# Decay table times span states in three rounded products, with table and states in two parts and one table for both tiles

## The chip, the cores and the metric

The kernel runs on one core of one Trainium2 chip. The metric is the device time in microseconds (us), the median of several runs. Beside it stands one execution that the hardware profiler recorded; all rows below come from that one.

## What is computed

Eight sequences of 1024 tokens with 512 channels pass two layers, both added to their input. The part that matters here is the second layer's decayed sum: eight causal moving averages with their own decay, each over gated values with its own modulation, blended per channel.

```python
ctx = causal_ema(x, tau_ctx)
gate_in = jnp.concatenate([x, ctx], axis=-1)
wg = jax.nn.sigmoid(jnp.einsum('btc,ec->bte', gate_in, Wg) + bg)
gated = x * wg
...
mod = 0.5 + jax.nn.sigmoid(jnp.einsum('bth,dh->btd', h1, Wn2) + bn2)
traces = jax.vmap(lambda tau, m: causal_ema(gated * m[..., None], tau))(tau_raws, jnp.moveaxis(mod, -1, 0))
blend_w = jax.nn.softmax(blend, axis=0)
temporal = jnp.einsum('dbtc,dc->btc', traces, blend_w)
gate = jax.nn.sigmoid(jnp.einsum('btc,ec->bte', temporal, Wtemp) + btemp)
soma = jax.nn.gelu(jnp.einsum('btc,ec->bte', x, Wsoma) + bsoma, approximate=False)
out = jnp.einsum('btc,ec->bte', soma * gate, Wout)
```

## The kernel before

The work is cut into 16 tiles of 512 tokens, two per sequence: the even one is the first half, the odd one the second half. A loop over slots k from -1 to 16 is written out on every engine. In slot k the tile k-1 is finished ("prev": temporal gate, output product, norm), tile k is in the middle ("cur"), and tile k+1 goes through the first layer ("next"). Each engine runs its instructions in the order in which `slot(k)` writes them, and semaphores join them. So the order is hand-written, and no scheduler moves anything.

Large products are done with both operands split in two rounded parts of type fp32r, high and low: `split_product` issues high by high, high by low and low by high. The high part is made by ACT (a copy that rounds), the low part by DVE (value minus high part).

The decayed sum of a tile of four blocks of 128 tokens has two parts, which meet in the same PSUM bank `Tp[b % 2]`, for block b:

- `within_spans(b, hh)` (L1011): within spans of 32 tokens. DVE's `products(b, hh, c)` (L761) multiplies the gated values, repeated over the partitions in `grep`, by blend weights into `U`. PE multiplies that by the decay matrices `Arep`.
- `from_before(b)` (L1020): what the span states bring in from before. `span_states` on PE (L993) writes one state per span and decay (16 x 8 = 128 rows) into the bank `smp`. DVE's `span_states` (L776) weights them by `w_jd` into `V`. PE multiplies the table `Epow` by `V` as plain fp32, one product for each block.

`tile_state` (L1026), in even tiles alone, makes the state that goes over to the odd tile. ACT copies it to `V[1][96:128]` (L514). There are two `V` buffers and 2 x 4 blocks of `Epow`: even and odd tiles have their own.

Then, for block b, ACT copies `Tp` out (`trace`, L492), PE transposes it (`trace_by_channels`, L1032), ACT makes the high part (`trace_high`, L436) and DVE the low one (`trace_low`, L649). With `trace_low(3)` the next slot's `temporal_gate` can begin; in a profile that is the product `ring<-seq_hi,Wtemp_hi`.

`grep` is loaded from memory, where SP's queue stores the gated values and reads them back four times per block (`repeat_spans`, L328). There are two buffers, so the load of block 3 waits until DVE has done the last product of block 1:

```python
                    if b >= 2:
                        sp.wait_ge(U_ready, upto(PIECES, k, 4 * (b - 2) + 3))
```

Of the kernel before, what the change touches and what calls it, by code (L numbers as in the profile page):

```python
# [4 lines left out]
P = 128  # L5
BATCHES, SEQ, C = 8, 1024, 512
A = 128
D = 8
# [3 lines left out]
NB = TOK // P  # L12
NC = C // P
L = 32
# [3 lines left out]
SPANS = TOK // L  # L18
LEVELS = 10
# [13 lines left out]
AT_EMASK = AT_EBITS + 5  # L33
# [7 lines left out]
def cond_resid_kernel(nc, x, xc, ids, w1, w2, b1, b2, g0, be0, wg, wn1, wsoma, wtemp, wout, wn2,  # L41
# [10 lines left out]
    with ctx:  # L52
        def sb(name, shape, dt=F):
            return ctx.enter_context(nc.sbuf_tensor(name, shape, dt))
# [10 lines left out]
        def sem(name):  # L65
            return ctx.enter_context(nc.semaphore(name))
# [31 lines left out]
        w_jd = sb("w_jd", [P, C])  # L98
        Dpow = sb("Dpow", [P, NH, L])
        Rpow = sb("Rpow", [P, NI, D])  # L100
        Epow = sb("Epow", [P, 2 * NB, P])
        Eend = sb("Eend", [P, 2 * (L - D) + D])

        grep = [sb(f"grep_{n}", [P, NI, C]) for n in range(2)]
        x_t = grep[0]
# [16 lines left out]
        V = [sb(f"V_{n}", [P, C]) for n in range(2)]  # L122
        soma, soma_lo = sb_two_ways("soma", [P, NC, TOK])
        stats0, stats1 = (V[0][:, at:at + 6 * NB].rearrange("p (b s) -> p b s", s=6)
                          for at in (128, 160))
        mv0, mv1 = (V[0][:, at:at + 2 * NB].rearrange("p (b s) -> p b s", s=2) for at in (192, 208))
# [12 lines left out]
        alpha = V[0][:, 0:LEVELS * ALS].rearrange("p (n a) -> p n a", a=ALS)  # L139
        alpha_1 = V[0][:, 128:128 + LEVELS * ALS].rearrange("p (n a) -> p n a", a=ALS)  # L140
        Qpow, Tpow = V[0][:, 256:288], V[0][:, 288:320]
        factors = g[:, :, :].rearrange("p n c -> p (n c)")[:, 0:5 * 4 * L].rearrange("p (n a t) -> p n a t", n=5, a=4)
        factors_s = V[0][:, 320:320 + 5 * D].rearrange("p (n d) -> p n d", n=5)
        factors_e = V[0][:, 384:389]
        blend_c = V[1][:, 0:NC * D].rearrange("p (n d) -> p n d", d=D)
        blend_s = V[1][:, 64:64 + NC]

        blend_x = ema.rearrange("p n t -> p (n t)")[:, 0:3 * NC * P].rearrange("p (a n c) -> p a n c", a=3, n=NC)

# [32 lines left out]
        split_lo = [sem(f"split_lo{n}") for n in range(6)]  # L182
        setup_step = sem("setup_step")
        blend_ready = sem("blend_ready")
        tables_ready = sem("tables_ready")
        sg_ready, ln1_step = sem("sg_ready"), sem("ln1_step")
        y_ready, ln0_step, x1_ready = sem("y_ready"), sem("ln0_step"), sem("x1_ready")
# [6 lines left out]
        rstd0_ready, rstd1_ready = sem("rstd0_ready"), sem("rstd1_ready")  # L194
        res_ready = sem("res_ready")
        xb2_ready, xbeta_ready, x1b_ready = sem("xb2_ready"), sem("xbeta_ready"), sem("x1b_ready")

        def upto(per_tile, tile, j):

            return tile * per_tile + (j + 1)  # L200
# [214 lines left out]
        def _(act):  # L415
            def split(n):

                act.wait_ge(ld_split[n], 16)
                hi, lo, raw = halves[n]
                nc.scalar.activation(hi, raw, ACT.Identity).then_inc(split_hi, 1)  # L420

            def slot(k):
                has_prev, has_cur, has_next = parts_of(k)

                def soma_gelu(e):
                    act.wait_ge(full["soma"], upto(4, k, e))
                    nc.scalar.activation(soma[:, e, :], bank_of("soma", k, e)[:, :], ACT.Gelu,
                                         bias=col[:, 1 + e:2 + e]).then_inc(soma_ready, 1)
# [57 lines left out]
                def open_gate(b):  # L486
                    act.wait_ge(pre_ready, upto(4, k, b))
                    nc.scalar.activation(g[:, b, :], g[:, b, :], ACT.Sigmoid).then_inc(sig_ready, 1)  # L488

                def trace(b):  # L490
                    act.wait_ge(full["T"], upto(4, k, b))
                    nc.scalar.activation(T_sb[b % 2][:, :], Tp[b % 2][:, :], ACT.Identity).then_inc(T_ready, 1)  # L492

                if has_cur:
                    open_gate(0)
                    act.wait_ge(m_pre, upto(1, k, 0))
                    nc.scalar.activation(m_nat, m_nat, ACT.Sigmoid).then_inc(msig_ready, 1)
                    if k == 0:
                        split(4)
                        split(5)  # L500
                    for b in range(1, NB):
                        open_gate(b)
                    soma_gelu(1)
                    trace(0)
                    soma_gelu(2)
                    trace(1)
                    trace_high(0)
                    trace(2)
                    trace_high(1)
                    soma_gelu(3)  # L510
                    if not k & 1:

                        act.wait_ge(full["carry"], k // 2 + 1)
                        nc.scalar.activation(V[1][96:128, :], smp[96:128, :], ACT.Identity).then_inc(carry_ready, 1)  # L514
                if k == -1:
                    split(0)
                    split(1)
                    split(2)
                if has_cur:
                    trace(3)  # L520
                if has_next:
                    x1_high(0)
                if has_cur:
# [21 lines left out]
        def _(dve):  # L545
            steps = [0]

            def link(ins):

                steps[0] += 1  # L550
                ins.then_inc(setup_step, 1)
                dve.wait_ge(setup_step, steps[0])
# [31 lines left out]
            def decay_tables():  # L584
# [18 lines left out]
                link(V_.memset(Eend[:, :], 0.0))  # L603
# [4 lines left out]
                for n in range(1, 5):  # L608
# [5 lines left out]
                V_.tensor_scalar(Eend[:, L - D:L], con[:, AT_EMASK:AT_EMASK + D], power_e, None, ALU.mult)  # L614
                V_.tensor_tensor(Qpow, power[:, 3, :], con[:, AT_QMASK:AT_QMASK + 32], ALU.mult)
                link(V_.tensor_scalar(Tpow, power[:, 0, :], alpha[:, 0, AL_JD:AL_JD + 1], None, ALU.mult))
                V_.tensor_tensor(Epow[:, :, :].rearrange("p x (i t) -> p (x i) t", t=L), Qpow.unsqueeze(2).to_broadcast([P, 32, L]),
                                 Tpow.unsqueeze(1).to_broadcast([P, 32, L]), ALU.mult)
# [5 lines left out]
            def slot(k):  # L624
# [146 lines left out]

                def span_states():

                    rows = slice(0, P - D if odd else P)
                    dve.wait_ge(full["S"], upto(1, k, 0))
                    V_.tensor_tensor(V[odd][rows, :], smp[rows, :], w_jd[rows, :], ALU.mult).then_inc(V_ready, 1)  # L776

                if has_cur:
                    if k == 0:
# [22 lines left out]
                                     ALU.mult).then_inc(A_ready, 1)  # L802
                    if k == 0:
                        split(4)
                    gate_logits(2)
                    gated(2)
                    dve.wait_ge(A_ready, upto(1, k, 0))
# [40 lines left out]
        def _(pe):  # L848
# [14 lines left out]
            def slot(k):  # L863
# [99 lines left out]
                def modulation():  # L963

                    pe.wait_ge(h1_ready, upto(1, k, 0))
                    if has_prev:
                        pe.wait_ge(V_ready, upto(1, k - 1, 0))
                        if odd:
                            pe.wait_ge(carry_ready, (k + 1) // 2)
# [44 lines left out]

                def from_before(b):

                    if b == 0 and k == 0:
                        pe.wait_ge(tables_ready, 1)
# [141 lines left out]
```

## Time and profile before

| | us |
|---|---|
| median of 3 runs | 1423.78 |
| lowest and highest | 1421.12, 1425.09 |
| the profiled execution, its own time | 1424.65 |
| its span in the profile | 1422.9 |

| engine | busy us | share of the span | instructions |
|---|---|---|---|
| PE (matmul) | 1344.8 | 95% | 7836 |
| DVE | 1010.4 | 71% | 1493 |
| ACT | 512.6 | 36% | 812 |
| POOL | 379.0 | 27% | 295 |

The profiled execution is 0.87 us above the median. The TensorE clock granted over the span was 0.987 of full speed. PE's busy time overlaps with itself, since matmuls are pipelined: a product of 128x512 is shown with 0.39 us while the next begins 0.23 us after it. A plain fp32 product of that size shows as two matmul records.

### The profile page before, as it was taken

What the parts mean: (1) busy time and instruction counts of PE and PEld (TensorE: products, weight loads), DVE (VectorE), ACT (ScalarE), POOL (GpSimd) and SP (SyncE); (2) the same over time, 40 slices, a digit from 0 to 9 for tenths busy, and PEclk for the clock granted to TensorE, in tenths of its full rate; (3) what the DMA queues carried; (4) which work ended last, traced back from release to release, by engine and by line L of the source; (5) the groups of instructions that cost most, each with busy time, mean ns of one, the idle gap of its engine ahead of it and who ended that gap; (6) DMA issues with size and microseconds to landing.
All of it is one profiled execution on the core that took longest, in us unless ns stands there. A gap on an engine that the chain in (4) does not pass through costs nothing.

```text
span 1422.9 us, 19538 instructions
## 1 busy us (share of the span) xinstructions
PE 1344.8 (95%) x7836; PEld 974.6 (68%) x7836; DVE 1010.4 (71%) x1493; ACT 512.6 (36%) x812; POOL 379.0 (27%) x295
## 2 busy tenths in 40 slices
PE   3599999999999999999999999999999999999995
PEld 2376857677586776858677685767758677686854
DVE  6967677676777867777776767767677786767463
ACT  2324234252333424234242433425233343423422
POOL 4414223041330514124041422304123051421102
PEclk8799999999999999999999999999999999999999
DMA  7345361735528173361715636173451816334250
GB/s 254 118 119 185 91 176 48 209 106 138 158 70 226 39 180 117 111 195 68 200 58 148 185 85 182 45 202 117 132 165 61 229 45 167 130 105 133 74 134 30
DMA packets 91484, 186.22 MB, mean 131 GB/s; under 512 B 9858, under 2 KB 14594, under 8 KB 87298
## 3 DMA queue, kind: packets, MB, share of 16 engines
q1 hardware_dynamic: 91394, 184.98, 44.8%
q8 instruction: 62, 1.02, 0.3%
q14 instruction: 28, 0.23, 0.1%
HBM read 134.61 MB, written 50.33 MB: 130 GB/s over the span
## 4 chain that ended last, share of the span: by engine, by line
PE 74%; DVE 9%; ACT 4%; DMA 4%; issue 3%; POOL 1%; SPq 1%; POOLq 0%; DVEq 0%
PE ring L859 56%; PE Tp L1011 6%; DVE U L761 5%; PE Tp L1020 4%; PE ring L852 3%; PE Tp L859 2%; DMA g_blocks<-g_f 2%; DVE seq_lo L649 2%; ACT T_sb_f L492 2%; PE smp L974 1%; DVE x1T_lo L631 1%; PE smp L993 1%; ACT seq_hi L436 1%; DMA grep<-g_blocks 1%; SPq L328 1%
## 5 line engine op out<-in xcount | busy, mean ns | idle before, releaser
L761 DVE TENSOR_TENSOR U<-grep,w_qs 128x1024 f32<-128x1024 f32 x256 | 298.4, 1219 | 6.6 <-DMA grep<-g_blocks 6.6
L382 POOL TENSOR_TENSOR x<-grep,b_row 128x512 f32<-128x512 f32 x64 | 80.5, 1289 | 603.3 <-DMA grep<-in_x 603.3
L1011 PE MATMUL Tp<-U,Arep 128*32 128x256 f32 x2048 | 146.5, 386 | 15.3 <-DVE U L761 14.8
L766 DVE TENSOR_TENSOR g_f<-ring,bg_row 128x512 f32<-128x512 f32 x64 | 44.2, 691 | 133.8 <-PE ring L859 133.8
L488 ACT ACTIVATE g_f<-g_f 128x512 f32<-128x512 f32 x64 | 40.5, 632 | 264.9 <-DVE g_f L766 264.8
L1011 PEld LDWEIGHTS Tp<-U,Arep 128*32 128x32 f32 x2048 | 52.7, 109 | 104.3 <-DVE U L761 44.8
L391 POOL TENSOR_TENSOR grep<-grep,beta_row 128x512 f32<-128x512 f32 x64 | 80.9, 1296 | 156.1 <-DMA grep<-x_tiles 156.1
L859 PE MATMUL ring<-seq_hi,Wtemp_hi 128*128 128x512 f32 x256 | 106.8, 417 | 8.5 <-DVE seq_lo L649 8.5
L492 ACT ACTIVATE T_sb_f<-Tp 128x512 f32<-128x512 f32 x64 | 38.2, 597 | 209.8 <-PE Tp L1020 209.8
L859 PE MATMUL ring<-Wg_hi,seq_hi 128*128 128x512 f32 x256 | 100.7, 393 | 9.1 <-DVE Wg_r L560 9.1
L859 PE MATMUL ring<-x1T_hi,Wsoma_hi 128*128 128x512 f32 x256 | 106.7, 417 | 0.0
L859 PE MATMUL ring<-Wg_hi,x1T_hi 128*128 128x512 f32 x256 | 103.4, 404 | 0.0
L859 PE MATMUL ring<-Wout_hi,g_r 128*128 128x512 f32 x256 | 99.8, 390 | 3.2 <-DVE soma_r L657 3.2
L859 PE MATMUL ring<-Wg_r,seq_hi 128*128 128x512 f32 x256 | 100.5, 393 | 0.0
L859 PE MATMUL ring<-Wg_hi,seq_lo 128*128 128x512 f32 x256 | 100.5, 393 | 0.0
L859 PE MATMUL ring<-x1T_hi,Wsoma_r 128*128 128x512 f32 x256 | 100.4, 392 | 0.0
L859 PE MATMUL ring<-Wg_hi,x1T_lo 128*128 128x512 f32 x256 | 100.0, 391 | 0.0
L859 PE MATMUL ring<-seq_hi,Wtemp_r 128*128 128x512 f32 x256 | 99.9, 390 | 0.0
L859 PE MATMUL ring<-x1T_lo,Wsoma_hi 128*128 128x512 f32 x256 | 99.9, 390 | 0.0
L859 PE MATMUL ring<-Wg_r,x1T_hi 128*128 128x512 f32 x256 | 99.7, 390 | 0.0
L859 PE MATMUL ring<-seq_lo,Wtemp_hi 128*128 128x512 f32 x256 | 99.7, 389 | 0.0
L859 PE MATMUL ring<-Wout_r,g_r 128*128 128x512 f32 x256 | 99.6, 389 | 0.0
(151 smaller groups left out, 2823.6 us busy)
## 6 DMA issues: line engine op xcount, KB each, us to landing
grep<-g_blocks SPq DMA_DIRECT2D x256, 256.0 KB, 4.4
grep<-in_xc SPq DMA_DIRECT2D x16, 1024.0 KB, 7.4
grep<-in_x SPq DMA_DIRECT2D x16, 1024.0 KB, 8.1
x_tiles<-x SPq DMA_DIRECT2D x16, 1024.0 KB, 7.6
g_blocks<-g_f SPq DMA_DIRECT2D x64, 256.0 KB, 4.6
grep<-x_tiles SPq DMA_DIRECT2D x16, 1024.0 KB, 4.8
out<-U SPq DMA_DIRECT2D x64, 256.0 KB, 2.0
gamma_row<-in_g SPq DMA_DIRECT2D x9, 256.0 KB, 7.6
```

Source lines behind the costliest of these rows:

```text
L328: sp.dma_start(grep[b % 2][q * L:(q + 1) * L, :, :], g_dram[b].rearrange("(i s) c -> s i c", i=NI)).then_inc(grep_in[b % 2], 16)
L382: nc.gpsimd.tensor_tensor(new[:, b, :], x_t[:, b, :], b2_row[:, :], ALU.add).then_inc(xb2_ready, 1)
L391: nc.gpsimd.tensor_tensor(x1_back[:, b, :], x1_back[:, b, :], beta1_row[:, :], ALU.add).then_inc(x1b_ready, 1)
L488: nc.scalar.activation(g[:, b, :], g[:, b, :], ACT.Sigmoid).then_inc(sig_ready, 1)
L492: nc.scalar.activation(T_sb[b % 2][:, :], Tp[b % 2][:, :], ACT.Identity).then_inc(T_ready, 1)
L649: V_.tensor_tensor(seq[1][:, :, at], bank_of("tt", k, b)[:, :].rearrange("p (n t) -> p n t", n=NC), seq[0][:, :, at].bitcast(F), ALU.subtr ...
L761: V_.tensor_tensor(U[:, (n + 2) % 4, :, :], grep[b % 2][:, :, at], w_qs[:, hh, at].unsqueeze(1).to_broadcast([P, NI, HC]), ALU.mult).then_ ...
L766: V_.tensor_tensor(g[:, b, :], bank_of("wg", k, b)[:, :], bg_row[:, :], ALU.add).then_inc(pre_ready, 1)
L852: last = nc.tensor.matmul(dst, lhsT(n), rhs(n), start=(n == 0), stop=(n == steps - 1))
L859: last = nc.tensor.matmul(dst, lhsT(a, n), rhs(b, n), start=(first and n == begin and m == 0), stop=(final and n == steps - 1 and m == 2))
L1011: last = nc.tensor.matmul(Tp[b % 2][i * L:(i + 1) * L, at], Arep[:, b * NI + i, hh, :], U[:, (n + 2) % 4, i, :], start=(hh == 0 and c == 0 ...
L1020: nc.tensor.matmul(Tp[b % 2][:, :], Epow[:, odd * NB + b, :], V[odd][:, :], start=False, stop=True).then_inc(full["T"], 1)
```

## The change

`Epow` and `Eend` (now 128 columns wide) are built as plain fp32 and split once, in slots -1 and 0, into high and low parts. Only one set of four `Epow` blocks is kept. DVE weights the span states in place in `smp`; ACT rounds them to `V_hi` (`states_high`), and DVE subtracts (`states_low`) into `V_lo`. `from_before` and `tile_state` become three fp32r products each. The copy of the tile state on ACT stands behind `trace(3)` now, in front of `x1_high(0)`, and DVE's `carry_low` is added at the end of an even tile's slot. The small statistics get a buffer of their own.

```diff
-        Epow = sb("Epow", [P, 2 * NB, P])
-        Eend = sb("Eend", [P, 2 * (L - D) + D])
+        Epow_raw, Epow_lo = sb_two_ways("Epow", [P, NB, P])
+        Epow = [sb("Epow_hi", [P, NB, P], R), Epow_lo]
+        Eend_raw, Eend_lo = sb_two_ways("Eend", [P, P])
+        Eend = [sb("Eend_hi", [P, P], R), Eend_lo]
...
+        def state_rows(tile):
+
+            return slice(0, P - D if tile & 1 else P)
+
+        def earlier_rows(tile):
+
+            return slice(0, P if tile & 1 else P - D)
...
+                def states_high():
+                    rows = state_rows(k)
+                    act.wait_ge(V_ready, upto(1, k, 0))
+                    nc.scalar.activation(V_hi[rows, :], smp[rows, :], ACT.Identity).then_inc(Vhi_ready, 1)
...
                     soma_gelu(1)
+                    states_high()
                     trace(0)
...
                     soma_gelu(3)
-                    if not k & 1:
-
-                        act.wait_ge(full["carry"], k // 2 + 1)
-                        nc.scalar.activation(V[1][96:128, :], smp[96:128, :], ACT.Identity).then_inc(carry_ready, 1)
...
+                    act.wait_ge(tables_ready, 1)
+                    nc.scalar.activation(Epow[0][:, :, :], Epow_raw[:, :, :], ACT.Identity).then_inc(tablehi_ready, 1)
+                    nc.scalar.activation(Eend[0][:, :], Eend_raw[:, :], ACT.Identity).then_inc(tablehi_ready, 1)
                 if has_cur:
                     trace(3)
+                    if not k & 1:
+
+                        act.wait_ge(full["carry"], k // 2 + 1)
+                        nc.scalar.activation(V_hi[96:128, :], smp[96:128, :], ACT.Identity).then_inc(carry_ready, 1)
                 if has_next:
                     x1_high(0)
...
-                    rows = slice(0, P - D if odd else P)
+                    rows = state_rows(k)
                     dve.wait_ge(full["S"], upto(1, k, 0))
-                    V_.tensor_tensor(V[odd][rows, :], smp[rows, :], w_jd[rows, :], ALU.mult).then_inc(V_ready, 1)
+                    V_.tensor_tensor(smp[rows, :], smp[rows, :], w_jd[rows, :], ALU.mult).then_inc(V_ready, 1)
+
+                def states_low():
+
+                    rows = state_rows(k)
+                    dve.wait_ge(Vhi_ready, upto(1, k, 0))
+                    V_.tensor_tensor(V_lo[rows, :], smp[rows, :], V_hi[rows, :].bitcast(F), ALU.subtract).then_inc(Vlo_ready, 1)
+
+                def carry_low():
+
+                    dve.wait_ge(carry_ready, k // 2 + 1)
+                    V_.tensor_tensor(V_lo[96:128, :], smp[96:128, :], V_hi[96:128, :].bitcast(F),
+                                     ALU.subtract).then_inc(carrylo_ready, 1)
...
                     if k == 0:
                         split(4)
+                        dve.wait_ge(tablehi_ready, 2)
+                        V_.tensor_tensor(Epow[1][:, :, :], Epow_raw[:, :, :], Epow[0][:, :, :].bitcast(F),
+                                         ALU.subtract).then_inc(tablelo_ready, 1)
+                        V_.tensor_tensor(Eend[1][:, :], Eend_raw[:, :], Eend[0][:, :].bitcast(F),
+                                         ALU.subtract).then_inc(tablelo_ready, 1)
...
                     products(1, 0, 0)
+                    states_low()
                     products(1, 0, 1)
...
+                if has_cur and not odd:
+                    carry_low()
...
-                    pe.wait_ge(V_ready, upto(1, k, 0))
-                    nc.tensor.matmul(Tp[b % 2][:, :], Epow[:, odd * NB + b, :], V[odd][:, :],
-                                     start=False, stop=True).then_inc(full["T"], 1)
+                    pe.wait_ge(Vlo_ready, upto(1, k, 0))
+                    for m, (a, c) in enumerate(((0, 0), (0, 1), (1, 0))):
+                        last = nc.tensor.matmul(Tp[b % 2][:, :], Epow[a][rows, b, :], V[c][rows, :], start=False, stop=(m == 2))
+                    last.then_inc(full["T"], 1)
...
-                    nc.tensor.matmul(smp[96:128, :], Eend[:, 0:L], V[0][:, :], start=True, stop=True).then_inc(full["carry"], 1)
+                    for m, (a, c) in enumerate(((0, 0), (0, 1), (1, 0))):
+                        last = nc.tensor.matmul(smp[:, :], Eend[a][:, :], V[c][:, :], start=(m == 0), stop=(m == 2))
+                    last.then_inc(full["carry"], 1)
```

On DVE, where an even tile's span states are weighted, before:

```order
L770 TENSOR_TENSOR g_f<-g_f,x_0 128x512
L776 TENSOR_TENSOR V<-smp,w_jd 128x512
L761 TENSOR_TENSOR U<-grep,w_qs 128x1024 x6
L649 TENSOR_TENSOR seq_lo<-ring,seq_hi 128x4x128
L761 TENSOR_TENSOR U<-grep,w_qs 128x1024 x4
```

and now:

```order
L795 TENSOR_TENSOR g_f<-g_f,x_0 128x512
L801 TENSOR_TENSOR smp<-smp,w_jd 128x512
L786 TENSOR_TENSOR U<-grep,w_qs 128x1024
L807 TENSOR_TENSOR V_lo_r<-smp,V_hi_r 128x512
L786 TENSOR_TENSOR U<-grep,w_qs 128x1024 x5
L674 TENSOR_TENSOR seq_lo<-ring,seq_hi 128x4x128
L786 TENSOR_TENSOR U<-grep,w_qs 128x1024 x4
```

One subtraction stands between the first and the second product of block 1; five products stand behind it ahead of `trace_low(0)`.

On PE, the last block of an even tile and what follows it, before:

```order
L1011 MATMUL Tp<-U,Arep 32x256 x8
L1026 MATMUL smp<-V,Eend 32x512
L1011 MATMUL Tp<-U,Arep 32x256 x8
L1020 MATMUL Tp<-V,Epow 128x512
L879 MATMUL ring<-ident,x_1 128x128 x4
```

and now:

```order
L1056 MATMUL Tp<-U,Arep 32x256 x8
L1074 MATMUL smp<-V_hi_r,Eend_hi 128x512
L1074 MATMUL smp<-V_lo_r,Eend_hi 128x512
L1074 MATMUL smp<-V_hi_r,Eend_r 128x512
L1056 MATMUL Tp<-U,Arep 32x256 x8
L1067 MATMUL Tp<-V_hi_r,Epow_hi 128x512
L1067 MATMUL Tp<-V_lo_r,Epow_hi 128x512
L1067 MATMUL Tp<-V_hi_r,Epow_r 128x512
L924 MATMUL ring<-ident,x_1 128x128 x4
```

One fp32 product became three fp32r products, twice; nothing else moved on PE.

On ACT, the end of an even tile's block work, now (before, the 32x512 copy stood ahead of the row of L512):

```order
L442 ACTIVATE soma_f<-ring,columns 128x512 [waits soma_full]
L512 ACTIVATE T_sb_f<-Tp 128x512 [waits T_full]
L544 ACTIVATE V_hi_r<-smp 32x512 [waits carry_full]
L447 ACTIVATE x1T_hi<-ring 128x512 [waits trx_full]
L451 ACTIVATE seq_hi<-ring 128x4x128 [waits tt_full] x2
```

The copy of the carried state stands between `trace(3)` and `x1_high(0)`.

## Rows read from the trace of the kernel before

**Rows 1.** The page, busy time, share of the span and instructions

```profile
PE 1344.8 (95%) x7836; PEld 974.6 (68%) x7836; DVE 1010.4 (71%) x1493; ACT 512.6 (36%) x812; POOL 379.0 (27%) x295
```

**Rows 2.** Waits, whole span: us in total, times, longest us

```profile
PE Tp L1011 <- DVE U L761: 14.8, 33, 1.0
...
DVE U L761 <- DMA grep<-g_blocks: 6.6, 12, 1.5
```

**Rows 3.** Chain that ended last, inside slot 8: start us, us, what

```profile
734.62 19.04 PE ring L859 x84
```

**Rows 4.** PE timeline, tile 6: start, us, instruction, [idle before <-releaser]

```profile
609.34 1.02 PE L1020 MATMUL Tp<-V,Epow 128*128 128x512 f32 x2
610.28 1.07 PE L1011 MATMUL Tp<-U,Arep 128*32 128x256 f32 x16
...
616.37 0.50 PE L859 MATMUL ring<-x1T_hi,Wsoma_hi 128*128 128x512 f32 x1
616.70 0.39 PE L859 MATMUL ring<-x1T_lo,Wsoma_hi 128*128 128x512 f32 x1
...
625.60 1.12 PE L1020 MATMUL Tp<-V,Epow 128*128 128x512 f32 x2
626.57 0.60 PE L879 MATMUL ring<-ident,x 128*128 128x128 f32 x4
...
629.92 0.47 PE L859 MATMUL ring<-seq_hi,Wtemp_hi 128*128 128x512 f32 x1 [0.47 <-DVE seq_lo L649]
```

**Rows 5.** DVE timeline, the same tile

```profile
607.11 0.69 DVE L776 TENSOR_TENSOR V<-smp,w_jd 128x512 f32<-128x512 f32 x1 [2.18 <-PE smp L993]
607.72 6.89 DVE L761 TENSOR_TENSOR U<-grep,w_qs 128x1024 f32<-128x1024 f32 x6
616.16 0.69 DVE L649 TENSOR_TENSOR seq_lo<-ring,seq_hi 128x512 fp32r<-128x512 f32 x1 [1.54 <-ACT seq_hi L436]
...
619.61 2.36 DVE L761 TENSOR_TENSOR U<-grep,w_qs 128x1024 f32<-128x1024 f32 x2 [0.49 <-DMA grep<-g_blocks]
622.02 0.69 DVE L649 TENSOR_TENSOR seq_lo<-ring,seq_hi 128x512 fp32r<-128x512 f32 x1
622.63 2.35 DVE L761 TENSOR_TENSOR U<-grep,w_qs 128x1024 f32<-128x1024 f32 x2
```

**Rows 6.** ACT timeline, the same tile

```profile
610.39 0.60 ACT L492 ACTIVATE T_sb_f<-Tp 128x512 f32<-128x512 f32 x1 [4.48 <-PE Tp L1020]
...
621.39 0.59 ACT L436 ACTIVATE seq_hi<-ring 128x512 fp32r<-128x512 f32 x1
...
624.61 0.59 ACT L514 ACTIVATE V<-smp 32x512 f32<-32x512 f32 x1 [1.17 <-PE smp L1026]
626.77 0.60 ACT L492 ACTIVATE T_sb_f<-Tp 128x512 f32<-128x512 f32 x1 [1.57 <-PE Tp L1020]
627.26 0.59 ACT L432 ACTIVATE x1T_hi<-ring 128x512 fp32r<-128x512 f32 x1
```

**Rows 7.** SP's queue, the same tile: the load of block 3

```profile
612.42 1.73 SPq L328 DMA_DIRECT2D grep<-g_blocks  x4
```

**Rows 8.** DVE timeline, tiles 8 and 13, where loads of `grep` came later

```profile
776.18 0.69 DVE L776 TENSOR_TENSOR V<-smp,w_jd 128x512 f32<-128x512 f32 x1 [2.18 <-PE smp L993]
...
789.32 2.36 DVE L761 TENSOR_TENSOR U<-grep,w_qs 128x1024 f32<-128x1024 f32 x2 [1.14 <-DMA grep<-g_blocks]
...
1205.22 2.36 DVE L761 TENSOR_TENSOR U<-grep,w_qs 128x1024 f32<-128x1024 f32 x2 [0.74 <-DMA grep<-g_blocks]
```

**Rows 9.** PE timeline, tile 8, the next slot's first product

```profile
799.49 0.47 PE L859 MATMUL ring<-seq_hi,Wtemp_hi 128*128 128x512 f32 x1 [0.47 <-DVE seq_lo L649]
```

**Rows 10.** DVE timeline, slot 7: the low part of `hid`

```profile
641.18 0.69 DVE L674 TENSOR_TENSOR T_sb_r<-ring,T_sb_r 128x512 fp32r<-128x512 f32 x1 [0.36 <-ACT T_sb_r L458]
```

**Rows 11.** PE timeline, slot 7: the first product that reads it

```profile
644.38 0.40 PE L859 MATMUL ring<-W_hi,T_sb_r 128*128 128x512 f32 x1
```

**Rows 12.** DVE timeline, tile 0: the last gated values

```profile
98.09 0.69 DVE L770 TENSOR_TENSOR g_f<-g_f,x 128x512 f32<-128x512 f32 x1
```

More of the change, by code:

```diff
@@ L121, in cond_resid_kernel @@
         m_rep = U[:, 3, NI - 1, 64:64 + NB * NI * NH].rearrange("p (x h) -> p x h", h=NH)
-        V = [sb(f"V_{n}", [P, C]) for n in range(2)]
+        spare0, V_hi = sb_two_ways("V_hi", [P, C])
+        spare1, V_lo = sb_two_ways("V_lo", [P, C])
+        V = [V_hi, V_lo]
+        stats = sb("stats", [P, 16 * NB])
         soma, soma_lo = sb_two_ways("soma", [P, NC, TOK])
-        stats0, stats1 = (V[0][:, at:at + 6 * NB].rearrange("p (b s) -> p b s", s=6)
-                          for at in (128, 160))
-        mv0, mv1 = (V[0][:, at:at + 2 * NB].rearrange("p (b s) -> p b s", s=2) for at in (192, 208))
+        stats0, stats1 = (stats[:, at:at + 6 * NB].rearrange("p (b s) -> p b s", s=6)
+                          for at in (0, 6 * NB))
+        mv0, mv1 = (stats[:, at:at + 2 * NB].rearrange("p (b s) -> p b s", s=2) for at in (12 * NB, 14 * NB))
         rows4 = sb("rows4", [P, 4, NB])
@@ L138, in cond_resid_kernel @@
         con = spare[:, 0:BITS]
-        alpha = V[0][:, 0:LEVELS * ALS].rearrange("p (n a) -> p n a", a=ALS)
-        alpha_1 = V[0][:, 128:128 + LEVELS * ALS].rearrange("p (n a) -> p n a", a=ALS)
-        Qpow, Tpow = V[0][:, 256:288], V[0][:, 288:320]
+        alpha = spare0[:, 0:LEVELS * ALS].rearrange("p (n a) -> p n a", a=ALS)
+        alpha_1 = spare0[:, 128:128 + LEVELS * ALS].rearrange("p (n a) -> p n a", a=ALS)
+        Qpow, Tpow = spare0[:, 256:288], spare0[:, 288:320]
         factors = g[:, :, :].rearrange("p n c -> p (n c)")[:, 0:5 * 4 * L].rearrange("p (n a t) -> p n a t", n=5, a=4)
[L143 to L146, printed above, removed]
+        factors_s = spare0[:, 320:320 + 5 * D].rearrange("p (n d) -> p n d", n=5)
+        factors_e = spare0[:, 384:389]
+        blend_c = spare1[:, 0:NC * D].rearrange("p (n d) -> p n d", d=D)
+        blend_s = spare1[:, 64:64 + NC]
         blend_x = ema.rearrange("p n t -> p (n t)")[:, 0:3 * NC * P].rearrange("p (a n c) -> p a n c", a=3, n=NC)
@@ L184, in cond_resid_kernel @@
         blend_ready = sem("blend_ready")
+        tablehi_ready, tablelo_ready = sem("tablehi_ready"), sem("tablelo_ready")
+        Vhi_ready, Vlo_ready, carrylo_ready = sem("Vhi_ready"), sem("Vlo_ready"), sem("carrylo_ready")
         tables_ready = sem("tables_ready")
@@ L602, in decay_tables @@
                 V_.tensor_tensor(factors_e, alpha_1[:, 5:10, AL_JD], con[:, AT_EBITS:AT_EBITS + 5], ALU.mult)
-                link(V_.memset(Eend[:, :], 0.0))
+                link(V_.memset(Eend_raw[:, :], 0.0))
                 power, power_s, power_e = factors[:, 0, :, :], factors_s[:, 0, :], factors_e[:, 0:1]
@@ L613, in decay_tables @@
                                  con[:, AT_DMASK:AT_DMASK + L].unsqueeze(1).to_broadcast([P, NH, L]), ALU.mult)
-                V_.tensor_scalar(Eend[:, L - D:L], con[:, AT_EMASK:AT_EMASK + D], power_e, None, ALU.mult)
+                V_.tensor_scalar(Eend_raw[:, P - D:P], con[:, AT_EMASK:AT_EMASK + D], power_e, None, ALU.mult)
                 V_.tensor_tensor(Qpow, power[:, 3, :], con[:, AT_QMASK:AT_QMASK + 32], ALU.mult)
                 link(V_.tensor_scalar(Tpow, power[:, 0, :], alpha[:, 0, AL_JD:AL_JD + 1], None, ALU.mult))
-                V_.tensor_tensor(Epow[:, :, :].rearrange("p x (i t) -> p (x i) t", t=L), Qpow.unsqueeze(2).to_broadcast([P, 32, L]),
-                                 Tpow.unsqueeze(1).to_broadcast([P, 32, L]), ALU.mult)
+                V_.tensor_tensor(Epow_raw[:, :, :].rearrange("p x (i t) -> p (x i) t", t=L),
+                                 Qpow[:, SPANS:2 * SPANS].unsqueeze(2).to_broadcast([P, SPANS, L]),
+                                 Tpow.unsqueeze(1).to_broadcast([P, SPANS, L]), ALU.mult)
                 V_.tensor_tensor(Rpow[:, :, :], power_s.unsqueeze(1).to_broadcast([P, NI, D]),
@@ L966, in modulation @@
                     if has_prev:
-                        pe.wait_ge(V_ready, upto(1, k - 1, 0))
+                        pe.wait_ge(Vlo_ready, upto(1, k - 1, 0))
                         if odd:
-                            pe.wait_ge(carry_ready, (k + 1) // 2)
+                            pe.wait_ge(carrylo_ready, (k + 1) // 2)
                     else:
@@ L1015, in from_before @@
                 def from_before(b):
+                    rows = earlier_rows(k)
                     if b == 0 and k == 0:
-                        pe.wait_ge(tables_ready, 1)
-                    pe.wait_ge(V_ready, upto(1, k, 0))
-                    nc.tensor.matmul(Tp[b % 2][:, :], Epow[:, odd * NB + b, :], V[odd][:, :],
-                                     start=False, stop=True).then_inc(full["T"], 1)
+                        pe.wait_ge(tablelo_ready, 2)
+                    pe.wait_ge(Vlo_ready, upto(1, k, 0))
+                    for m, (a, c) in enumerate(((0, 0), (0, 1), (1, 0))):
+                        last = nc.tensor.matmul(Tp[b % 2][:, :], Epow[a][rows, b, :], V[c][rows, :], start=False, stop=(m == 2))
+                    last.then_inc(full["T"], 1)
                 def tile_state():
-                    nc.tensor.matmul(smp[96:128, :], Eend[:, 0:L], V[0][:, :], start=True, stop=True).then_inc(full["carry"], 1)
+                    for m, (a, c) in enumerate(((0, 0), (0, 1), (1, 0))):
+                        last = nc.tensor.matmul(smp[:, :], Eend[a][:, :], V[c][:, :], start=(m == 0), stop=(m == 2))
+                    last.then_inc(full["carry"], 1)
                 def trace_by_channels(b):
```

## The prediction

> **What bounds the kernel now.** The page comes first: PE is busy 95% of the span, DVE 71%, ACT 36% [rows 1]. That reads as a kernel in which each product taken from PE is time won, and for most of a slot it is. In the chain that ended last, 84 rounded products in one piece take 19.04 us, 0.227 us each, with no gap [rows 3]. But the products of this change stand in another stage, so the second view is the table of waits, and the third the timelines of one tile, engine by engine.
>
> The waits show that PE does wait inside the blocks: 33 times for DVE's products into `U`, 14.8 us in all, and DVE waits 12 times for the repeated values `grep`, 6.6 us in all [rows 2]. The timelines show a ring of short steps there. In tile 6 it reads so. `from_before(1)` ends, ACT copies it and makes a high part, DVE waits 1.54 us for that and makes the low part at 616.16 [rows 5]. Two products into `U` follow. Then DVE waits 0.49 us for block 3 of `grep`, whose load SP issued at 612.42, right when DVE had finished the last product of block 1 [rows 5, 7]. Two more products, 2.36 us, and at 622.02 the low part of block 1, which ACT's high part (621.39 plus 0.59) allows at that same moment [rows 5, 6]. Then the last two products, which end at 624.98 [rows 5], PE's eight small products, `from_before(3)` at 625.60, ACT's copy at 626.77, `x1_high(0)` at 627.26, DVE's low parts, and PE's next slot at 629.92 after a wait of 0.47 us [rows 4, 6]. From 616 on, the length of the stage is this ring's latency. PE's spare work (the `soma` products, transposes, `tile_state`) fills its gaps and doesn't set the end.
>
> So a late block 3 must lengthen the slot, and a row shows it. In tile 8 DVE waited 1.14 us for it instead of 0.49. The next slot's first product began at 799.49, 23.31 us after the span states (776.18) [rows 8, 9]; in tile 6 that distance is 629.92 less 607.11, 22.81 [rows 4, 5]. Of 0.65 us later, 0.50 came out at the end.
>
> **The change part by part.**
>
> PE's products. A plain fp32 product took 0.94 us from its start to the next one's (609.34 to 610.28) [rows 4]. No row shows the three new ones, but rows of the same shape and type do: 0.33 us to the second one after small products (616.37 to 616.70), then 0.23 each [rows 3, 4], so 0.79 us. That is 0.15 less on PE's queue. In latency, 1.12 us of the fp32 pair at 625.60 becomes 0.33 + 0.23 + 0.39 = 0.95, so 0.17 less; I take 0.16.
>
> `from_before(0)`. It waited for `V` on DVE; now it waits for ACT's `V_hi` and DVE's `V_lo`. ACT is free: it was idle for 4.48 us ahead of 610.39 [rows 6], so its 0.60 us lie beside DVE's first product of block 1. DVE starts the subtraction at 607.72 plus a sixth of 6.89, that is 608.9, and it takes 0.69 like the others: 609.6, where PE wanted it at 609.34 [rows 4, 5]. So PE loses 0.3 there and gets back 0.15 from this product and 0.16 from the next. Up to `trace(1)` that is nothing. `from_before(2)` gives 0.16 more, but what it releases waits for DVE, as follows.
>
> `states_low` on DVE. It pushes five products by 0.61 us (the step from 607.11 to 607.72) [rows 5]. Ahead of `trace_low(0)` the 1.54 us of idle time cover it [rows 5]. Not covered is the queue of SP: the load of block 3 waits for the last product of block 1, so its four DMAs go out 0.61 later in each tile [rows 7]. How much comes out? Without a wait DVE could start block 3 at 619.61 - 0.49 = 619.12 and come to `trace_low(1)` 2.3 us later, at 621.4; ACT lets it start at 622.02. The slack is 0.62 [rows 5]. So a tile in which DVE already waits w gets later by the smaller of w and 0.61, and a tile that doesn't wait by nothing. The waits sum to 6.6 us [rows 2]. One of 0.74 stands before block 2 [rows 8] and doesn't count. The longest, 1.5, and the 1.14 count 0.61 each [rows 2, 8]. That leaves 6.6 - 0.7 - 0.9 - 0.5 = **+4.5**. Bounds: nothing if the load lands as before, 16 x 0.61 = 9.8 if every tile pays in full.
>
> `from_before(3)`. It follows that delay on the ring and is the one of the four whose saving counts: 16 x 0.16 = **-2.6**. Bounds 0 and 16 x 0.3.
>
> The carry's copy on ACT. Before, it lay at 624.61 and ACT still had 1.57 us of idle time behind it [rows 6]. Now it stands between `trace(3)` and `x1_high(0)`, which followed each other in 0.49 us [rows 6]. Behind it in ACT's queue are `x1_high(0)` and the high parts of blocks 2 and 3; for these wait DVE's low parts, and for the last of them PE's next slot. The copy's 0.59 is as long as a full one's [rows 6], so it costs a step of 0.49 in eight even tiles: **+3.9**. Bounds: 0 and 8 x 0.6.
>
> `tile_state`: three products for one, in a gap of PE while DVE works on the last two products. Nothing. If that cover were gone, 0.15 in eight tiles would be won.
>
> `carry_low` on DVE, at the end of eight slots, 0.61 us ahead of `soma_gated(0)`. Behind it waits the low part of `hid`: it ended at 641.87 and PE wanted it at 644.38, 2.5 us of cover [rows 10, 11]. Nothing; 8 x 0.6 = 4.9 if the cover were gone.
>
> Setup. The table's build shrinks by half, while PE waits for loads and other work: nothing. In slot 0 DVE makes the low tables, one of 512 and one of 128 columns, about 0.8 us, ahead of `gate_logits(2)`. The last gated values ran with no idle time before them [rows 12], and PE's span states need them. Bounds 0 and 0.8; I take **+0.6**.
>
> The sum: 4.5 - 2.6 + 3.9 + 0.6 = +6.4 us. Against the profiled execution's 1424.65 that is 1431.1; against the median, 0.87 lower, 1430.2.
>
> **The rivals.** (a) PE sets the pace everywhere: 64 products give 0.15 each and 8 `tile_state` the same, -10.8 us, 1413. For it speaks the 95% of rows 1; against it the waits inside the stage, and that the slot with a later load was longer although PE's work was equal [rows 8, 9]. The Trainium skill, page "Perfetto Trace Analysis", section "Identifying the Most-Contended Engine", says to take the engine with the highest occupancy first, and by it this would be the result; the same section says that matmul busy time is a poor measure for PE, and the trace agrees, with 0.39 us shown for a product that costs 0.227. The chance is 9%.
>
> (b) The load of block 3 lands as early as before, because its start later falls in a calmer stretch, or its delay is caught elsewhere. The 4.5 goes and 1.9 stays: 1425.7. For it: the wait differs from tile to tile between nothing and 1.5 us, so landing isn't only a matter of the issue. 18%.
>
> (c) The covers of DVE are thinner than they look, and `carry_low` or the later start of the next slot's loads reach PE: 8 x 0.61 more, 1435. It decides once more than 2.5 us of DVE's cover are used up elsewhere. 10%.
>
> (d) The three products don't take less time than the fp32 one, since weights of 128 columns must be loaded three times. Then the -2.6 goes: 1432.8. Against it: products with as many weights follow at 0.227. 7%.
>
> My forecast, with its own range 1427 to 1434: 56%.
>
> **How the numbers follow.** A change of 0.3%, 4.3 us, is about what a measurement of this kernel tells from none: 1419.5 to 1428.1. Slower: most of the forecast (0.50), (c) and (d), 0.66. The same: (b) and the low end of the forecast, 0.23. Faster: (a) and a little for what I overlook, 0.11. The range goes from 1423 (below (b), in case that ACT's copy costs less too) to 1436 (above (c)).
>
> **What would show it.** In the profile after: `from_before` as three products 0.23 apart; in a tile's timeline DVE's wait for `grep` before block 3 where there was none or longer by up to 0.6; in even tiles the copy of 32x512 between the copies of `Tp` and `x1`; from span states to the next slot's first product some 23.3 us in even tiles and 22.9 to 23.1 in odd ones, against 22.81. PE's busy share falls while the span grows. It is wrong if those distances shrink, or if the load of block 3 isn't issued later.

## The result: 1454.4 us, slower by 2.1%

The changed kernel takes 1454.43 us (median of 4 runs, 1449.82 to 1454.65) against 1423.94 before. The ratio is 1.0211, with a 95% interval from 1.0196 to 1.0227. The interval begins just below 2%. The direction was forecast, the size was not: +30 us instead of +6. The profiled execution is the fastest of the four, 1449.82 us with a span of 1448.0.

The page after, busy times and the costliest group, which answer to [rows 1, 2]:

```profile
PE 1359.1 (94%) x7908; PEld 985.4 (68%) x7908; DVE 1021.0 (71%) x1519; ACT 524.9 (36%) x830; POOL 376.7 (26%) x295
...
L786 DVE TENSOR_TENSOR U<-grep,w_qs 128x1024 f32<-128x1024 f32 x256 | 299.9, 1218 | 14.0 <-DMA grep<-g_blocks 14.0
```

DVE's wait for `grep` grew from 6.6 to 14.0 us. PE is busy for 14 us more, although plain fp32 work was taken from it. The timelines of tile 6 after, PE first, then DVE, ACT and SP's queue, answer to [rows 4 to 7]:

```profile
616.15 0.49 PE L1067 MATMUL Tp<-V_hi_r,Epow_hi 120*128 120x512 f32 x1
616.49 0.39 PE L1067 MATMUL Tp<-V_lo_r,Epow_hi 120*128 120x512 f32 x1
616.72 0.40 PE L1067 MATMUL Tp<-V_hi_r,Epow_r 120*128 120x512 f32 x1
617.04 1.07 PE L1056 MATMUL Tp<-U,Arep 128*32 128x256 f32 x16
...
632.28 0.50 PE L1067 MATMUL Tp<-V_hi_r,Epow_hi 120*128 120x512 f32 x1
...
637.18 0.47 PE L904 MATMUL ring<-seq_hi,Wtemp_hi 128*128 128x512 f32 x1 [1.22 <-DVE seq_lo L674]
```

```profile
613.67 0.70 DVE L801 TENSOR_TENSOR smp<-smp,w_jd 128x512 f32<-128x512 f32 x1 [2.27 <-PE smp L1038]
614.28 1.22 DVE L786 TENSOR_TENSOR U<-grep,w_qs 128x1024 f32<-128x1024 f32 x1
615.41 0.69 DVE L807 TENSOR_TENSOR V_lo_r<-smp,V_hi_r 128x512 fp32r<-128x512 f32 x1
616.01 5.76 DVE L786 TENSOR_TENSOR U<-grep,w_qs 128x1024 f32<-128x1024 f32 x5
622.75 0.69 DVE L674 TENSOR_TENSOR seq_lo<-ring,seq_hi 128x512 fp32r<-128x512 f32 x1 [0.98 <-ACT seq_hi L451]
...
626.42 2.36 DVE L786 TENSOR_TENSOR U<-grep,w_qs 128x1024 f32<-128x1024 f32 x2 [0.72 <-DMA grep<-g_blocks]
```

```profile
633.27 0.60 ACT L512 ACTIVATE T_sb_f<-Tp 128x512 f32<-128x512 f32 x1 [3.41 <-PE Tp L1067]
633.90 0.59 ACT L544 ACTIVATE V_hi_r<-smp 32x512 fp32r<-32x512 f32 x1
634.51 0.60 ACT L447 ACTIVATE x1T_hi<-ring 128x512 fp32r<-128x512 f32 x1
```

```profile
619.57 1.73 SPq L343 DMA_DIRECT2D grep<-g_blocks  x4
```

The block stage looks as the prediction drew it. The three products are 0.34 and 0.23 us apart. `states_low` stands behind the first product of block 1 and takes 0.60 to the next. The load of block 3 goes out 5.90 us after the span states instead of 5.31 [rows 5, 7]. The carried state's copy stands in the ACT chain. From the span states (613.67) to the next slot's first product (637.18) it is 23.51 us, against 22.81 [rows 4, 5]. In the odd tile behind it, it is less than before, where 22.9 to 23.1 was expected:

```profile
700.21 0.70 DVE L801 TENSOR_TENSOR smp<-smp,w_jd 120x512 f32<-120x512 f32 x1 [2.27 <-PE smp L1038]
```

```profile
722.87 0.47 PE L904 MATMUL ring<-seq_hi,Wtemp_hi 128*128 128x512 f32 x1 [0.47 <-DVE seq_lo L674]
```

That is 22.66 us. Summed over 16 tiles, this distance is 372.5 us after and 365.9 before: +6.6, where my terms for this stage gave 4.5 - 2.6 + 3.9 = +5.8.

The rest lies where the diff adds almost nothing: from a slot's first product to the next tile's span states. Only behind an even tile is there one instruction more, `carry_low`. Between 637.18 and 700.21 it is 63.03 us; before, from 629.92 [rows 4] to 691.64, the start of tile 7's span states, 61.72. The 15 such stretches sum to 940.4 us after and 920.0 before, +20.4. Of these, 14 are longer by 1.3 to 1.4 each, behind odd tiles as much as behind even ones, so `carry_low` isn't the cause. The last one is longer by 1.85. Tile 7's span states in the DVE timeline of the kernel before:

```profile
691.64 0.69 DVE L776 TENSOR_TENSOR V<-smp,w_jd 120x512 f32<-120x512 f32 x1 [2.18 <-PE smp L993]
```

The chain after, in that stretch (start us, us, what), answers to [rows 3]:

```profile
637.18 5.83 PE ring L904 x24
...
657.64 19.60 PE ring L904 x84
```

84 rounded products take 19.60 us instead of 19.04: 0.2333 each instead of 0.2267, without a gap. TensorE's granted clock over the span was 0.988, as before (0.987). Nothing waits here. The same products on the same data are slower.

### The profile page after: what moved, and what is told of

It is laid out like the page before. It is cut to its first block, busy times and chain, and to the rows that moved or that the text cites. A ratio compares the mean times of both kernels' runs of the same rounds, so it can differ in the third digit from the quotient of the medians.

```text
span 1448.0 us, 19726 instructions
## 1 busy us (share of the span) xinstructions
PE 1359.1 (94%) x7908; PEld 985.4 (68%) x7908; DVE 1021.0 (71%) x1519; ACT 524.9 (36%) x830; POOL 376.7 (26%) x295
## 4 chain that ended last, share of the span: by engine, by line
PE 68%; DVE 15%; DMA 6%; issue 3%; ACT 2%; SPq 1%; POOL 1%; POOLq 0%; DVEq 0%
PE ring L904 56%; DVE U L786 10%; DMA grep<-g_blocks 6%; PE ring L897 3%; PE Tp L904 3%; PE Tp L1056 2%; DVE seq_lo L674 2%; PE Tp L1067 1%; SPq L343 1%; PE smp L1038 1%; PE smp L1019 1%; DVE x1T_lo L656 1%; ACT T_sb_f L512 1%; DVE V_lo_r L807 1%; ACT x1T_hi L447 1%
## 5 line engine op out<-in xcount | busy, mean ns | idle before, releaser
L1056 PE MATMUL Tp<-U,Arep 128*32 128x256 f32 x2048 | 143.5, 386 | 18.6 <-DVE U L786 18.1
L512 ACT ACTIVATE T_sb_f<-Tp 128x512 f32<-128x512 f32 x64 | 38.3, 598 | 184.7 <-PE Tp L1067 184.7
L904 PE MATMUL ring<-Wout_hi,soma_r 128*128 128x512 f32 x256 | 101.3, 396 | 0.0
```

The costliest lines, as they stand in the source:

```text
L904: last = nc.tensor.matmul(dst, lhsT(a, n), rhs(b, n), start=(first and n == begin and m == 0), stop=(final and n == steps - 1 and m == 2))
L1056: last = nc.tensor.matmul(Tp[b % 2][i * L:(i + 1) * L, at], Arep[:, b * NI + i, hh, :], U[:, (n + 2) % 4, i, :], start=(hh == 0 and c == 0 ...
```

## The experiments

What differs in them? Not their number, shape or order, but where their operands lie. The built programs' allocations (start in bytes within a partition, and its remainder by 64):

```
buffer      before          changed
Wg_hi       17536,  0       17536,  0
Wsoma_hi    46208,  0       46208,  0
x1T_hi     153984,  0      154784, 32
seq_hi     170368,  0      171168, 32
g_r        191360,  0      192160, 32
soma_r     220032,  0      221088, 32
```

The new tables take 5120 bytes where `Epow` and `Eend` took 4320. Everything behind them moved by 800 bytes, and `soma`, which also has the new statistics buffer ahead of it, by 1056. Neither is a multiple of 64. My theory (A): a rounded product one of whose operands starts 32 bytes past a multiple of 64 costs 0.2333 us, otherwise 0.2267. The rival (B): the added work slows PE down in some other way.

**1. The changed kernel with even addresses.** `bn2_row`, 32 bytes, is allocated last.

```diff
-        bn2_row = sb("bn2_row", [P, D])
...
         rows4 = sb("rows4", [P, 4, NB])
+        bn2_row = sb("bn2_row", [P, D])
```

> The changed kernel with one thing else: the 32-byte row bn2_row is allocated last, so every large buffer behind it starts on a multiple of 64 bytes again (in the changed kernel all buffers behind Epow start 32 bytes past one, in the kernel before they start on one). Theory A, the start address: the rounded products outside the block stage come at 0.227 us again instead of 0.233, some 1.3 us in each of 16 slots, and the time falls from 1454 to 1431 to 1435. Rival B, the added instructions and waits slow PE down whatever the addresses are: 1454 stays, and the products stay at 0.233.

Measured: 1430.32 us (1429.95 to 1434.84), ratio to the kernel before 1.0048 (1.0031 to 1.0065). That is just under the 1431 to 1435 expected, and 24 of the 30 us are gone with one line moved. The profiled execution is the slowest of the four, 1434.84 us. The chain shows 0.2267 again:

```profile
636.71 5.74 PE ring L904 x24
...
656.89 19.04 PE ring L904 x84
```

**2. The kernel before with odd addresses.** No instruction differs.

```diff
         Eend = sb("Eend", [P, 2 * (L - D) + D])
+        pad = sb("pad", [P, 8])
```

> The kernel before with an unused buffer of 32 bytes in front of grep, so that grep, T_sb, x1, x1T, seq, Arep, g, U, V and soma start 32 bytes past a multiple of 64, and no instruction differs. Theory A: 84 products in one piece take 19.6 us instead of 19.04, and the time rises by 20 to 23 us, to 1444 to 1448. Rival B: no change, 1424.

Measured: 1444.94 us, ratio 1.0156 (1.0135 to 1.0177), most of the loss without the change:

```profile
634.61 5.84 PE ring L860 x24
...
655.07 19.60 PE ring L860 x84
```

**3. The kernel before with the weights odd, the activations even.**

```diff
+        pad_first = sb("pad_first", [P, 8])
         Wg_raw, Wg_lo = sb_two_ways("Wg", [P, 2 * NC, C])
...
         Eend = sb("Eend", [P, 2 * (L - D) + D])
+        pad = sb("pad", [P, 8])
```

> The kernel before with 32 unused bytes in front of the weights and 32 in front of grep: now the weights Wg, Wn1, Wsoma, Wtemp and Wout start 32 bytes past a multiple of 64, and all activations on one. Theory A in its wide form (it is enough that one of the two operands is so placed): every product at 0.233 again, 1444 to 1448. Narrow form (only the operand that streams through the array counts): temp and soma, whose streamed operand is an activation, at 0.227, out and wg at 0.233, so about half the loss or a little more, 1434 to 1439. Rival B: 1424.

Measured: 1442.75 us, ratio 1.0135 (1.0114 to 1.0156). That is 1.3 us under the range of the wide form and well above that of the narrow one, and the products come at 0.2333. The wide form holds.

```profile
635.26 5.84 PE ring L861 x24
...
655.72 19.60 PE ring L861 x84
```

The 24 products are those of `temp`: they stream `seq`, even here, and hold `Wtemp`, odd here. In run 2 it was the other way round, with the same 5.84. It is enough that either operand is odd.

**4. The kernel before with everything even.** Run 1's line and run 2's pad together.

> The kernel before with bn2_row allocated last and 32 unused bytes in front of grep: weights and activations stay on multiples of 64, and W1, W2, the identity matrix, w_qs and Epow, which stood 32 bytes past one, come onto one too. Theory A: the 12 products of y in each slot go from 0.233 to 0.227, 0.08 us a slot, and little else, 1421 to 1424. Rival B: 1424. It is the partner of the first run: the difference of the two is the change without its shift of addresses, and my sum of the block stage gives +5 to +7 us for that.

Measured: 1424.36 us, ratio 1.0010 (0.9996 to 1.0023), no change. Run 1 lies 6.0 us above it, within the +5 to +7 expected for the change without its shift of addresses. The part on `y` was wrong: 36 products, 12 of them `y`, took 8.28 us with their operands even and 8.26 before. So these products are slow for another reason, which no run here looked for.

**5. The carried state's copy last on ACT,** in the kernel of run 1.

```diff
                     trace(3)
-                    if not k & 1:
-
-                        act.wait_ge(full["carry"], k // 2 + 1)
-                        nc.scalar.activation(V_hi[96:128, :], smp[96:128, :], ACT.Identity).then_inc(carry_ready, 1)
...
                     for n in range(1, NC):
                         x1_high(n)
+                if has_cur and not k & 1:
+                    act.wait_ge(full["carry"], k // 2 + 1)
+                    nc.scalar.activation(V_hi[96:128, :], smp[96:128, :], ACT.Identity).then_inc(carry_ready, 1)
```

> The changed kernel with even addresses (as in the first run) and ACT's copy of the carried state moved from between trace(3) and x1_high(0) to the end of ACT's slot. Theory: the copy's whole step lies on the path there, 0.75 us in eight even tiles (in the changed kernel the ACT copies around it start 0.63 and 0.61 us apart where 0.49 stood), so the time falls by 6 us, 1430.3 to 1424. By my forecast's term it would be 3.9 us. Rival: DVE's low parts wait for something else too, and nothing is won: 1430.

Measured: 1427.47 us, ratio 1.0024 (1.0002 to 1.0045). Against run 1's ratio that is some 3 us, with intervals of about 3 on either side. In the traces the 16 distances fall from 371.2 to 365.6, but 1.7 of that is tile 1, where a fall of the clock lengthened run 1's execution (more on it in run 8). The eight even tiles, which alone have the copy, fall by 4.7 us, and by 6.2 against the execution of run 10. The rival is out; neither the median nor the traces separate 3.9 from 6 here.

**6. One DVE instruction more in the kernel before.**

```diff
                     products(1, 0, 0)
+                    V_.tensor_tensor(V[odd ^ 1][:, :], smp[:, :], w_jd[:, :], ALU.mult)
                     products(1, 0, 1)
```

> The kernel before with one DVE multiplication more, of 128x512 from smp, between the first and the second product of block 1, its result unused. It is the cost of states_low alone: 0.61 us on DVE and a load of block 3 that is issued 0.61 later. By my forecast's term: +4.5 us, 1427.5 to 1428.5. Rival, which the trace after suggests (odd tiles were 0.15 us shorter there, just what the faster product gives): the load lands hardly later than before, less than +2 us, 1423 to 1425.

Measured: 1428.58 us, ratio 1.0036 (1.0020 to 1.0052), 5.1 us. The 16 distances sum to 370.0 against 365.9, +4.0. My term of 4.5 was right, and the rival that the trace after had suggested is out. DVE's waits, whole span (us in total, times, longest), against 6.6 before:

```profile
DVE U L761 <- DMA grep<-g_blocks: 15.5, 17, 1.4
```

**7. The carried state's copy behind `trace(3)` in the kernel before.**

```diff
-                    if not k & 1:
-
-                        act.wait_ge(full["carry"], k // 2 + 1)
-                        nc.scalar.activation(V[1][96:128, :], smp[96:128, :], ACT.Identity).then_inc(carry_ready, 1)
...
                     trace(3)
+                    if not k & 1:
+
+                        act.wait_ge(full["carry"], k // 2 + 1)
+                        nc.scalar.activation(V[1][96:128, :], smp[96:128, :], ACT.Identity).then_inc(carry_ready, 1)
```

> The kernel before with ACT's copy of the carried state behind trace(3) instead of ahead of it. Theory: 8 x 0.75 = +6 us, 1429. By my forecast's term: 8 x 0.49 = +3.9 us, 1427. If ACT's copies aren't on the path: 1423.

Measured: 1430.21 us, ratio 1.0039 (1.0023 to 1.0056), 5.6 us. ACT in tile 6:

```profile
628.24 0.60 ACT L492 ACTIVATE T_sb_f<-Tp 128x512 f32<-128x512 f32 x1 [3.33 <-PE Tp L1020]
628.86 0.59 ACT L520 ACTIVATE V<-smp 32x512 f32<-32x512 f32 x1
629.48 0.60 ACT L432 ACTIVATE x1T_hi<-ring 128x512 fp32r<-128x512 f32 x1
```

Two steps of 0.62 stand where one of 0.49 stood [rows 6]: +0.75. Six of the eight even tiles read 23.54 or 23.55 us instead of 22.81. All 16 distances sum to 372.2, +6.3.

**8. One product instead of three,** in the kernel of run 1.

```diff
-                    for m, (a, c) in enumerate(((0, 0), (0, 1), (1, 0))):
-                        last = nc.tensor.matmul(Tp[b % 2][:, :], Epow[a][rows, b, :], V[c][rows, :], start=False, stop=(m == 2))
+                    last = nc.tensor.matmul(Tp[b % 2][:, :], Epow[0][rows, b, :], V[0][rows, :], start=False, stop=True)
```

> The changed kernel with even addresses, and from_before does one of its three products, high by high (the two with low parts are left out, so the output lacks them). PE then has 64 x 0.46 = 29.4 us less to do than in the first run. Theory: only the fourth of a tile counts, in its latency: 16 x 0.46 = 7.4 us less, 1430.3 to 1423, perhaps one or two more where the second and third bring a tile's low parts forward. Rival, PE sets the pace of the block stage: 1401.

Measured: 1429.21 us, ratio 1.0031 (1.0014 to 1.0049). 29 us of PE's work are gone and some 2 us of time, with intervals of about 2.5 on either measurement. So the amount of PE's work doesn't set the pace of this stage. My 7.4 was there tile by tile: quiet even tiles read 22.81 to 22.83 us instead of the 23.3 to 23.4 of run 1. Two things took it back. First, the load of block 3 was waited for longer. DVE's waits for it, in this run and then in run 1:

```profile
DVE U L786 <- DMA grep<-g_blocks: 23.4, 16, 2.5
```

```profile
DVE U L786 <- DMA grep<-g_blocks: 11.0, 16, 1.4
```

Second, TensorE's granted clock fell to 0.50, the lower of its two levels (1.2 and 2.4 GHz). It did so behind such waits, when PE had run short of work. In tile 7 of this run, DVE's wait, and then PE busy and the granted clock by microsecond (start:end, length, busy us of PE, PEld, DVE, ACT and POOL, clock, DMA share, GB/s):

```profile
707.98 2.36 DVE L786 TENSOR_TENSOR U<-grep,w_qs 128x1024 f32<-128x1024 f32 x2 [2.51 <-DMA grep<-g_blocks]
```

```profile
711.00:712.00 1.00, 0.03 (x4) 0.00 (x0) 1.00 (x2) 0.00 (x0) 0.00 (x0) 1.00 0.12 45
713.00:714.00 1.00, 0.74 (x8) 0.16 (x8) 0.20 (x1) 0.00 (x0) 0.43 (x1) 0.69 0.01 4
714.00:715.00 1.00, 1.00 (x6) 0.61 (x3) 0.00 (x0) 0.00 (x0) 1.00 (x2) 0.50 0.15 53
715.00:716.00 1.00, 1.00 (x7) 1.00 (x6) 0.00 (x0) 0.70 (x2) 1.00 (x1) 0.50 0.82 293
```

The same is seen in tiles 3, 5 and 9. Together these four are 4.2 us longer than in run 1, while the other twelve are 6.1 shorter; 2.0 of the 6.1 is tile 1, where the clock fell in run 1's execution. It fell at the end of the last tile too, and what lies behind that tile's distance is 4.1 us longer than in run 1. Over the whole span the granted clock was 0.978 to 0.986 in the ten executions of this run, 0.985 to 0.988 in those of run 1. Run 8 rules its rival out, then, but how the small gain splits between the load and the clock wasn't tested.

**9. A new order in the block stage,** on top of run 5.

```diff
                     products(1, 0, 0)
-                    states_low()
                     products(1, 0, 1)
                     products(1, 1, 0)
                     products(1, 1, 1)
+                    states_low()
...
                     soma_begun(2)
-                    from_before(0)
                     within_spans(1, 0)
                     soma_ended(2)
                     within_spans(1, 1)
+                    from_before(0)
                     from_before(1)
...
+                    soma_gelu(2)
                     trace(0)
-                    soma_gelu(2)
                     trace(1)
```

> The changed kernel with even addresses and the carried state's copy last (as in the fifth run), and a new order in the block stage: DVE's states_low behind the last product of block 1, so the load of block 3 is issued as early as before the change; PE's from_before(0) behind within_spans(1, 1), right ahead of from_before(1); ACT's soma_gelu(2) ahead of trace(0). If the late load of block 3 is what eats the products' gain, the distance from the span states to the next slot's first product falls from 22.8 us to 22.3, and the time to 1415 to 1419, below the kernel before. Rival: the ring is bound elsewhere, or PE waits at the moved product: 1424 or more.

Measured: 1422.59 us, ratio 0.9976 (0.9961 to 0.9992). It beats both kernels, the one before by 0.24% alone, where I had expected 1415 to 1419. The three moves were made together, so their shares aren't known. The distances sum to 362.3 against 365.9 before; most read 22.64 to 22.67, not 22.3. The waits for `grep` are nearly gone:

```profile
DVE U L785 <- DMA grep<-g_blocks: 1.0, 2, 0.7
```

Why 22.65? In tile 8 (span states at 777.93), `from_before(0)` ends so late that ACT copies both `Tp` banks in one go, and DVE waits for the high part of block 0:

```profile
785.11 1.29 ACT L512 ACTIVATE T_sb_f<-Tp 128x512 f32<-128x512 f32 x2 [1.22 <-PE Tp L1066]
```

```profile
787.15 0.69 DVE L673 TENSOR_TENSOR seq_lo<-ring,seq_hi 128x512 fp32r<-128x512 f32 x1 [1.12 <-ACT seq_hi L451]
```

That low part begins 9.22 us after the span states, in a quiet tile of run 1 (tile 5, distance 22.53) after 9.09. So `from_before(0)`, moved right ahead of `from_before(1)`, is itself on the ring now. It explains 0.12 us by the traces; no run moved it back alone.

**10. Run 1 again, on the chip of run 9.**

> The kernel of the first run once more, on the same chip as the one above and with more rounds: 1429 to 1432, which settles what the change costs without its shift of addresses.

Measured: 1431.95 us, ratio 1.0045 (1.0030 to 1.0060). Without its shift of addresses the change costs 6.4 us (4.3 to 8.5).

## Why the prediction was wrong

**The step that failed** is one that the sum doesn't contain. "What bounds the kernel now" read the 84 products in one piece as 0.227 us each, and every part of the sum took it that products outside the block stage stay as they are. The change to the tables was costed as work in the setup ("the table's build shrinks by half ... nothing"), and never as a move of all that is allocated behind them. Runs 1 to 4 show what stands in its place: 0.0067 us more for a rounded product outside the block stage. In each of 14 stretches that made 1.3 to 1.4 us, what some 200 products give (tile 6's stretch holds 228 beside the 12 of `y`, so not quite all count). The 15 stretches hold 20.4 us of it, of which 0.9 has another cause (below); runs 2 and 3, without the change, hold 19.6 and 19.5. By the medians it is 24 us (1454.4 against 1430.3). Had the new buffers been a multiple of 64 bytes longer than the old ones, the 1430.3 of run 1 or the 1432.0 of run 10 would have come out, against a forecast of 1430.2.

That agreement is partly luck: two terms were too small, with opposite signs.

- `states_low` and the late load of block 3, +4.5: run 6 gives 5.1 (2.8 to 7.4), and 4.0 in its trace. Right.
- The carry's copy, +3.9: mis-sized. Run 7 gives 5.6 (3.3 to 8.0), and 0.74 a tile, 5.9, in the trace. I took the step of 0.49 between two copies of 128 partitions for that of any copy. Around the 32-partition one the copies don't overlap; the bound of 8 x 0.6 was too narrow.
- `from_before(3)`, -2.6: mis-sized too. Quiet odd tiles of runs 1 and 10 read 22.52 to 22.54 us against 22.80 or 22.81, so 0.28 and not 0.16. The 0.16 is there: from the product's start to ACT's copy it is 1.00 us (547.18 to 548.18, run 1) instead of 1.16 (710.14 to 711.30, before). The other 0.12 comes from `from_before(2)`, of which I said that what it releases waits for DVE. In tile 7 of the kernel before it was DVE that waited, for the high part of block 1, and in tile 5 of run 1 it doesn't:

```profile
706.55 0.69 DVE L649 TENSOR_TENSOR seq_lo<-ring,seq_hi 128x512 fp32r<-128x512 f32 x1 [0.31 <-ACT seq_hi L436]
```

```profile
543.60 0.69 DVE L674 TENSOR_TENSOR seq_lo<-ring,seq_hi 128x512 fp32r<-128x512 f32 x1
```

  At 0.28 in 16 tiles, -4.5, the three terms of this stage make 4.0 + 5.9 - 4.5 = +5.4 by the traces; run 10 has +5.7 (371.6 against 365.9).
- `carry_low`, `tile_state`, the build of the tables: 14 stretches behind the block stage are about as long in run 1 (61.7 us) as before. Nothing, as said, but for one: the last stretch is 56.96 us against 56.09, and 56.95 to 57.00 in all five runs with `carry_low` and even addresses. No next tile fills PE there, so `carry_low` (0.73 us to the next DVE instruction) reaches PE's wait for the gated `soma`, in run 1 and then before:

```profile
1330.49 0.50 PE L904 MATMUL ring<-Wout_hi,g_r 128*128 128x512 f32 x1 [1.24 <-DVE soma_r L682]
```

```profile
1321.62 0.50 PE L859 MATMUL ring<-Wout_hi,g_r 128*128 128x512 f32 x1 [0.39 <-DVE soma_r L657]
```

- Slot 0, +0.6: its block stage was longer by 1.3 us in run 1 (24.1 against 22.8), though runs 2 and 3, which add no work there, read 23.1 and 23.5. But the first span states began anywhere from 96.0 to 103.1 us in these profiles, whatever the kernel, so a term of that size in the setup can't be read from one execution.
- Rival (a), PE sets the pace everywhere, -10.8: ruled out for this stage by run 8. For the stretches, where the slower products came out in full or nearly so, it is true, and it is just there that the 20 us were lost. Rival (b), the load lands as early: ruled out by run 6. Rival (c), thin covers of DVE: true in the last stretch alone. Rival (d), three products as slow as one fp32: ruled out by the traces, where `from_before(3)` takes 0.81 us to PE's next instruction in run 1 (547.18 to 547.99) and 0.96 before (710.14 to 711.10).

What stays open: why a product slows down at an odd address at all; why `y` and the `soma` products in the block stage take 0.233 us with even operands too; how run 8's lost gain splits; and what happens at start addresses other than these two remainders.

## What to carry to other kernels

When an edit changes the size of a buffer, print the start address of everything allocated behind it, and compare it modulo 64 bytes before pricing any instruction; if a stretch without edits changes its length, look there first. An engine that is 95% busy can be the bound in one stage and filler in another, so price a saving in the stage in which it falls, and ask which transfer waits next. And look at the granted clock of a run from which work was taken: in run 8 it was lower than in run 1, so its time is not the edit's alone. Work that is put in front of the last reader of a double buffer delays the next load by its full length.

## What the runs showed of the hardware

- A 128x512 product of fp32r operands follows the one before it after 0.2267 us when both operands start on a multiple of 64 bytes, and after 0.2333 when the held one, the streamed one or both start 32 bytes past it: 19.04 against 19.60 us for 84, in the eight kernels with even addresses and the three with odd ones. That is 2.9% more for such a product at the full granted clock. It isn't the whole rule: the 12 products of `y`, and those of `soma` between the small products of the block stage, came at 0.233 with even addresses too.
- Copies on ACT of 128x512 from PSUM start 0.49 us apart. A copy of 32x512 between two of them makes that 0.62 on either side, so it costs 0.75 us.
- In run 8, tile 7, PE was busy for 0.03 us of one microsecond and partly idle around it; from 714 to 716 its granted clock was 0.50, at 717 it was back at 1.00. Work taken from PE in a stage that waits for a transfer bought such falls in four tiles and the last one.
